# One semaphore per ring slot, and a table stored pair by pair, in a graph network kernel

## The reference

```python
deg = segment_sum(ones, dst) + 1; dinv = rsqrt(deg)
h0 = dinv * (segment_sum(dinv[src] * x[src], dst) + dinv * x) @ W + b + t_emb @ Wt + bt
x = layernorm(x + h0)
mean(v) = segment_sum(v[src], dst) / max(cnt, 1)
h = relu(mean(x) @ Wl1.T + b1 + x @ Wr1.T)
x = layernorm(x + mean(h) @ Wl2.T + b2 + h @ Wr2.T)
```

## Time and profile before

| | |
|---|---|
| median of three runs | 3865.3 us (3864.66 to 3870.44) |
| the profiled execution's own time | 3868.9 us |
| its span, first to last instruction | 3867.1 us |
| first gather issued | 192.15 us |
| PE busy | 3067.6 us (79%) |
| DVE busy | 1094.8 us (28%) |
| ACT busy | 503.1 us (13%) |
| POOL busy | 2257.4 us (58%) |
| moved | 1102.5 MB, 285 GB/s over the span |

### The profile page before, as it was taken

One profiled execution on the slowest core, in us unless ns is written; L12 is line 12 of the kernel. 1 busy time (PEld: TensorE's weight loads), 2 busy tenths in 40 slices (PEclk: granted clock), 3 DMA queues, 4 the chain that ended last, 5 costly groups with the idle time before them and its releaser, 6 DMA issues.

```text
span 3867.1 us, 52767 instructions
## 1 busy us (share of the span) xinstructions
PE 3067.6 (79%) x11711; PEld 1400.9 (36%) x12104; DVE 1094.8 (28%) x1877; ACT 503.1 (13%) x1048; POOL 2257.4 (58%) x2367
## 2 busy tenths in 40 slices
PE   7156667778888878788989978886778889988888
PEld 7012223333333333333444433342334344433333
DVE  8701112222333431112222323332122222222222
ACT  0500000111112220000111111111000111111112
POOL 0066666666666636666666666654666666666663
PEclk9988878888899989899999989998889999999999
DMA  5587788888999968888889999987888888888785
GB/s 170 218 301 273 267 274 289 297 305 308 321 323 324 328 244 286 279 282 277 298 309 309 319 328 321 318 311 262 282 278 284 272 281 278 285 280 280 270 279 192
DMA packets 278572, 1102.52 MB, mean 285 GB/s; under 512 B 53626, under 2 KB 55196, under 8 KB 278514
## 3 DMA queue, kind: packets, MB, share of 16 engines
q0 software_dynamic: 187680, 922.63, 69.3%
q10 hardware_dynamic: 64638, 137.22, 10.0%
q1 hardware_dynamic: 26228, 42.34, 3.1%
HBM read 1003.75 MB, written 99.06 MB: 285 GB/s over the span
## 4 chain that ended last, share of the span: by engine, by line
PE 44%; another core or an unknown queue 20%; issue 19%; ACTq 6%; DVE 3%; ACT 3%; DMA 3%; POOL 2%; DVEq 0%; SPq 0%; POOLq 0%
PE sum_ps L1187 27%; PE root_ps L1195 8%; PE prod_ps L1195 7%; POOL raw L457 2%; DMA raw<-table,idx_ring 1%; ACTq L249 1%; PE selfT_ps L1209 1%; PE aggT_ps L1173 1%; ACT selfT L931 1%; ACTq L969 1%; DMA table<-stage 1%; DVE left_of L643 1%; DVE stage L635 1%; ACTq L272 1%
## 5 line engine op out<-in xcount | busy, mean ns | idle before, releaser
L457 POOL DMA_INDIRECT raw<-table,idx_ring x2346 | 2248.0, 958 | 1483.8 <-issue 834.8
L1187 PE MATMUL sum_ps<-raw,oh 128*128 128x512 bf16 x6682 | 1718.1, 402 | 516.4 <-issue 463.6
L1187 PEld LDWEIGHTS sum_ps<-raw,oh 128*128 128x128 bf16 x7038 | 696.1, 102 | 1434.3 <-issue 778.6
L765 DVE TENSOR_TENSOR oh<-iota_ps,dst_rel 128x1280 bf16<-128x1280 f32 x237 | 352.9, 1489 | 1438.5 <-remote 684.2
L1195 PE MATMUL prod_ps<-W,aggT 128*128 128x512 f32 x1176 | 547.4, 607 | 20.9 <-issue 11.8
L1195 PE MATMUL root_ps<-W,selfT 128*128 128x512 f32 x800 | 400.6, 644 | 72.3 <-issue 69.1
L1195 PEld LDWEIGHTS prod_ps<-W,aggT 128*128 128x128 f32 x1176 | 230.3, 197 | 265.9 <-issue 247.4
L887 ACT ACTIVATE aggT<-aggT_ps 128x512 f32<-128x512 f32 x147 | 87.7, 597 | 1827.0 <-remote 1359.9
L1187 PE MATMUL sum_ps<-raw,oh_next 128*128 128x512 bf16 x847 | 229.8, 401 | 37.7 <-issue 26.8
L1195 PEld LDWEIGHTS root_ps<-W,selfT 128*128 128x128 f32 x800 | 160.6, 206 | 270.2 <-issue 258.9
L924 ACT ACTIVATE selfT<-selfT_ps 128x512 f32<-128x512 f32 x100 | 59.7, 597 | 1004.3 <-remote 644.6
(11 more groups left out here) (149 smaller groups left out, 1156.5 us busy)
## 6 DMA issues: line engine op xcount, KB each, us to landing
raw<-table,idx_ring POOLq DMA_INDIRECT x2346
table<-planes ACTq DMA_DIRECT2D x89, 384.0 KB
selfbuf<-rows ACTq DMA_DIRECT2D x104, 256.0 KB
selfbuf<-table ACTq DMA_DIRECT2D x50, 384.0 KB
table<-stage SPq DMA_DIRECT2D x7, 2688.0 KB, 8.3
rows<-X ACTq DMA_DIRECT2D x49, 256.0 KB
X<-rows ACTq DMA_DIRECT2D x49, 256.0 KB
X<-in_x SPq DMA_DIRECT2D x6, 2048.0 KB
```

The costliest lines, as they stand in the source:

```text
L457: nc.gpsimd.indirect_dma_start(out=raw[:, n, j, :], out_offset=None, in_=tables[L][:, :], in_offset=bass.IndirectOffsetOnAxis(ap=idx_ring[ ...
L765: v.tensor_tensor(oh[:, which * HR:(which + 1) * HR, :, :].rearrange("p n j e -> p (n j) e"), iota_ps[:, 0:P].unsqueeze(1).to_broadcast([P ...
L1187: last = mm(bank, of[:, j, :], raw[:, n, j, p * D:(p + 1) * D], start=fresh, stop=False, skip_group_check=True)
```

## The change

1. `slot_read[n]` takes the place of `pe_done`: PE's last matmul of a group raises the semaphore of its slot, and POOL, DVE and ACT wait for that of the slot that they need.
2. PE waits for `slot_full[n]` itself; SP's loop and `gathered` are gone. `oh_made` is raised by 1 a half block, and PE waits for it at slots 0 and 5 only. ACT's index copy waits until PE has read slot 9 of its block (before: until that slot had landed).
3. The first table is stored in 28 DMAs, one after each of the 28 steps.
4. The edge tables are copied by ACT, after its step 15; the tile ends' counts come after DVE's step 11 and not 8, the column numbers after step 18, and the relative targets after the last step.
5. DVE makes the first one-hots before it waits for the stores. `dst_f` and `ended_f` move in SBUF to where `oh` lies, and `rel_f` is gone.
6. ACT takes a root of one column before it waits for the degrees; DVE's wait for POOL's last constants moves behind the copies that don't need them.

```diff
+            for n, (first, many) in enumerate(TWOS):
+                b, k = first // BT, first % BT
+                sp.wait_ge(S["staged"], n + 1)
+                sp.dma_start(tables[0][first * P:(first + many) * P, :].rearrange("(t p) (a d) -> p t a d", p=P, a=PLANES),
+                             stage[:, b % 2, k:k + many, :, :]).then_inc(stored[b % 2], 16)
...
-                def landed(blk, n):
-
-                    fills = NBLK + 1 if n == 0 else NBLK
-                    sp.wait_ge(slot_full[n], blk * (16 * CH) + 16 * CH * (fills * L + 1))
-                    sp.sem_inc(S["gathered"], 1)
...
-                        pool.wait_ge(S["pe_done"], blk * SLOTS + (REAL * L + n + 1))
+                        pool.wait_ge(slot_read[n], blk + (fills(n, L) + 1))
...
-            dve.wait_ge(S["consts_made"], 3)
             link(v.tensor_copy(cnt[:, :], hist_ps[:, 0:T]))
...
+            dve.wait_ge(S["consts_made"], 3)
...
-                if n == 12:
-                    edge_tables()
-                if n == 16:
-                    relative_targets()
+                if n == 11:
+                    tile_end_counts()
+                if n == 18:
+                    column_numbers()
             low_planes(len(TWOS) - 1)
+            relative_targets()
             dve.wait_ge(S["tabs_made"], 2)
-            dve.wait_ge(S["b0_all_ps"], 1)
-            dve.wait_ge(S["stage_stored0"], 16 * 4)
-            dve.wait_ge(S["stage_stored1"], 16 * 3)
...
-                half_block(0, slice(0, HR * CH), REAL * L + SLOTS)
+                half_block(0, slice(0, HR * CH), slot_read[0], fills(0, L) + 1)
+                if L == 0:
+                    dve.wait_ge(S["b0_all_ps"], 1)
+                    dve.wait_ge(S["stage_stored0"], 16 * 4 * PAIRS)
+                    dve.wait_ge(S["stage_stored1"], 16 * 3 * PAIRS)
...
             act.wait_ge(S["consts_made"], 1)
+            a.activation(sqsum[:, 0:1], eps[:, 0:1], ACT.Sqrt)
...
+            def edge_tables():
+
+                act.wait_ge(S["src_ps"], 1)
+                a.activation(idx_tab[:, 0:4 * CQ], tmp_ps[0][:, 0:4 * CQ], ACT.Copy)
+                a.activation(idx_tab[:, 4 * CQ:NC], tmp_ps[1][:, 0:NC - 4 * CQ], ACT.Copy).then_inc(S["tabs_made"], 1)
+                act.wait_ge(S["dst_ps"], 1)
+                a.activation(dst_f[:, 0:4 * CQ], tmp_ps[2][:, 0:4 * CQ], ACT.Copy)
+                a.activation(dst_f[:, 4 * CQ:NC], tmp_ps[3][:, 0:NC - 4 * CQ], ACT.Copy).then_inc(S["tabs_made"], 1)
...
-                    act.wait_ge(S["gathered"], b * SLOTS + (REAL * L + SLOTS))
+                    act.wait_ge(slot_read[SLOTS - 1], b + (fills(1, L) + 2))
                     next_indices(b % 2, (b + 2) % (NBLK + 1))
...
-                    pe.wait_ge(S["oh_made"], g + (HR * (NW + 1) * L + 1))
-                    pe.wait_ge(S["gathered"], g + (REAL * L + 1))
+                    if n % HR == 0:
+                        pe.wait_ge(S["oh_made"], b * (SLOTS // HR) + ((NW + 1) * L + n // HR + 1))
+                    pe.wait_ge(slot_full[n], b * (16 * CH) + 16 * CH * (fills(n, L) + 1))
```

More of the change, by code:

```diff
@@ L49, in gnn_resnorm @@
     TWOS = [(t, min(2, T // 7 - t % (T // 7))) for t in range(T) if t % (T // 7) % 2 == 0]
+    PAIRS = len(TWOS) // 7
+    assert len(TWOS) == 7 * PAIRS
     HB = 34
@@ L118, in gnn_resnorm @@
         mid = ExitStack()
+        dst_f = sb("dst_f", [P, NC], fp32, mid)
+        ended_f = sb("ended_f", [P, SB * P], fp32, mid)
+        assert 4 * (NC + SB * P) <= 2 * SLOTS * CH * P + 2 * CH * P
         stage = sb("stage", [P, 2, BT, PLANES, D], bf16, mid)
@@ L195, in gnn_resnorm @@
         slot_full = [sem(f"slot_full{n}") for n in range(SLOTS)]
+        slot_read = [sem(f"slot_read{n}") for n in range(SLOTS)]
         block = ctx.enter_context(nc.Block())
@@ L204, in tile_of_x, with fills @@
             return X2[:, bass.ds(t1 * D - D, D)]
+        def fills(n, L):
+            return L * (NBLK + (n == 0))
         def column(per_node, t1):
@@ L349, in _ @@
             stored = (S["stage_stored0"], S["stage_stored1"])
[L350 to L353, removed]
+            for n, (first, many) in enumerate(TWOS):
[3 more added lines that the diff above has]
+                             stage[:, b % 2, k:k + many, :, :]).then_inc(stored[b % 2], 16)
             sp.wait_ge(S["tabs_made"], 2)
             sp.wait_ge(S["b0_made"], 1)
-            sp.wait_ge(S["stage_stored0"], 16 * 4)
-            sp.wait_ge(S["stage_stored1"], 16 * 3)
+            sp.wait_ge(S["stage_stored0"], 16 * 4 * PAIRS)
+            sp.wait_ge(S["stage_stored1"], 16 * 3 * PAIRS)
             for L in range(NL):
@@ L385, in _ @@
                     load_weights(1, wr2t, "wr_loaded")
[L386 to L389, removed]
         @block.gpsimd
@@ L760, in tile_end, with half_block @@
                         dve.nop()
-                def half_block(which, cols, done):
-                    dve.wait_ge(S["pe_done"], done)
+                def half_block(which, cols, read, times):
+                    dve.wait_ge(read, times)
                     v.tensor_tensor(
@@ L867, in _ @@
                     middle_planes(n - 1)
+                if n == 15:
+                    edge_tables()
             middle_planes(len(TWOS) - 1)
@@ L1085, in _ @@
             pe.sem_inc(S["root_ready"], 1)
-            pe.sem_inc(S["pe_done"], SLOTS)
+            for n in range(SLOTS):
+                pe.sem_inc(slot_read[n], 1)
             pe.sem_inc(S["next_used"], 1)
@@ L1229, in groups, with group @@
                             each(pe, rounds[n // HR], rounds[n // HR + 1], lambda r: own_rows(L, r), T + 1)
-                        group(b * SLOTS + n, n, ends[n], ends[n + 1])
-                def group(g, n, first, end):
-                    pe.wait_ge(S["oh_made"], g + (HR * (NW + 1) * L + 1))
-                    pe.wait_ge(S["gathered"], g + (REAL * L + 1))
+                        group(b, n, ends[n], ends[n + 1])
+                def group(b, n, first, end):
+                    if n % HR == 0:
+                        pe.wait_ge(S["oh_made"], b * (SLOTS // HR) + ((NW + 1) * L + n // HR + 1))
+                    pe.wait_ge(slot_full[n], b * (16 * CH) + 16 * CH * (fills(n, L) + 1))
                     with pe.If(end > first):
@@ L1241, in group @@
                         mm(sums_of(L, end + 1, 1), zeros[:, :], zeros[:, 0:1], start=False, stop=False,
-                           skip_group_check=True).then_inc(S["pe_done"], 1)
+                           skip_group_check=True).then_inc(slot_read[n], 1)
                     with pe.Else():
-                        add_rows(sums_of(L, first + 1), oh[:, n, :, :], n, False).then_inc(S["pe_done"], 1)
+                        add_rows(sums_of(L, first + 1), oh[:, n, :, :], n, False).then_inc(slot_read[n], 1)
                     pe.nop()
@@ L1249, in _ @@
                 ends = ended_before(mybir.EngineType.PE, TAIL_GROUP, 1)
-                group(TAIL_GROUP, 0, ends[0], ends[1])
+                group(NBLK, 0, ends[0], ends[1])
                 weigh(L, T - 1)
```

46 lines of the change are left out of this document (16 added, 30 removed).

## The result

The changed kernel takes **3826.8 us** (3825.7 to 3830.7) against 3867.7 us (3864.7 to 3870.4) for the kernel before on the same chip: ratio 0.9891, 95% interval 0.9876 to 0.9906, so 41 us less. I had forecast 3850, 15.6 us less. The sign holds, and the time lies in the stated range of 3812 to 3872, but not in the forecast's own of 3838 to 3857: the gain is over twice the size.

A forecast was written before the change was run, and what follows sets the result against it. No engine was full: DVE bounded the plane loop, and in the layers engines waited for each other through ten slots. 1.6 + 10 + 4.0 = 15.6 us before the gathers and 0 in the layers gave 3850 us, range 3812 to 3872.

The forecast's parts named there:

- Front: Before the plane loop: early dummy Sqrt hides a 1.28 us table load, DVE's moved wait gives 0.35; sum 1.6 us.
- Plane loop: DVE making the first table's planes: stalls 4.2, tile counts 3.5, edge tables 2.0, relative targets 2.15; 11.85, taken as 10 us.
- Last store: Between last subtraction and first gather: only one tile's store follows the last pair, not a batch; gain 4.0 us, bounds 3 and 5.
- Before the gathers: Sum of front 1.6, plane loop 10 and last store 4.0: 15.6 us, between 10 and 18.
- The layers: Three layers of gathers after the first gather: relay, PE's waits, index copy and slot semaphores sum to 0, bounds -27 and +29.
- the ring: Ten gather slots shared by POOL and PE in the layers; their changed waits and semaphores were put at 0 us in sum.
- One wait less for PE: In eight of ten groups of the layers PE drops one event instruction, median 51 ns; taken as nothing.
- SP's relay: SP waited for each of 1173 groups and passed it on to PE; removing it was taken as 0 to 1 us.
- Rival 1: Layers: PE's shorter control path saves 27 us, giving 3823; sign: PE's unnamed waits below 465 us; chance 0.22.
- Rival 2: Block starts in the layers: POOL waits for ACT's index copy, 39 exposed starts cost 29 us, giving 3879; chance 0.12.
- Rival 3: Plane loop: stores per pair don't overlap, the last ends about 14 us later, giving 3880; chance 0.05.
- Rival 4: Layers: a different phase gives back as much as the early start gains, 3865, within 0.2%; chance 0.11.

The follow-up runs named there:

- kind A: Chips on which the kernel before takes 3833 to 3880 us, as on the one of the forecast.
- a store per batch: Changed kernel with the first table stored in seven batches of seven tiles, as before: 0.9927 of the kernel before, on a slow chip (3880.1 us before).
- the four waits: Changed kernel plus four waits on PE before every group, on semaphores reached long ago: 0.9932 of the kernel before, on a slow chip.
- kind B: Chips on which the kernel before takes 3323 to 3327 us.
- run 5: Not a run: in "seven batches that each run 5 to 6 us over 9.1", "run" is a verb and 5 to 6 us a time.
- the ring alone: Kernel before with only SP's relay, PE's waits, slot semaphores and index copy changed: 0.9995, 0.9998 and 1.0004 of the kernel before, on fast chips.
- the start alone: Kernel before with every edit ahead of the gathers and the old slot signalling: 0.9945, 0.9943 and 0.9947 of the kernel before, on fast chips.

## Why the prediction was right in sign and wrong in size

*Front, 1.6 us:* 1.8. The table load is gone from behind the histogram, and DVE's copy stands at 95.70, released by PE: 0.50 us earlier, where 0.35 was forecast. The other 1.3 are the load.

*Plane loop, 10 us:* 11.7. The three waits and the moved work are gone as named. What was mis-sized is the 1.6 us that I let come back as a stall on ScalarE's edge tables: the row at 140.93 has 0.29. 11.85 - 0.29 = 11.6. ScalarE itself waited 13.8 us for VectorE in the loop, so it had room for four copies, as its 53.26 busy us of 77.82 had said; I let the stall come back in spite of them. I also summed terms that hang together (stores and order), which was right only because both were changed.

*Last store, 4.0 us:* 4.5. The last landing released ACT at 173.17, 4.0 us after the last subtraction's end at 169.13; 4.3 was expected. The Trainium skill's *DMA: Bandwidth & Descriptors*, in the section on where the ~2 µs goes, gives a DMA a fixed cost of about 2 us, fitted there to DMAs that GpSimd issues, where these stores are SP's. By that rule with nothing overlapped 21 more stores would lose. The runs bear out the overlap: with 28 stores the first gather comes 13.1 us earlier than with seven, and a landing takes 2.4 to 3.4 us.

*Before the gathers, 15.6 (10 to 18):* 17.9, as the first gather shows, and all of it arrives at the end.

*The layers, 0:* 23 to 24 us on chips of kind A, in three comparisons (23.0 and 23.8 for the changed kernel, 24.0 with a store per batch). That these belong to the ring is inferred, from kernels that all have both parts: the start's part of each is the time of its first gather, and it arrives in full. A gain that needs ring and start together isn't excluded. **The step that failed is the zero for the layers**, and in it first this term: "*One wait less for PE* in eight of ten groups: its event instruction has a median of 51 ns, in a sequencer that runs ahead of the matmuls: I take nothing", together with the 0 to 1 us for SP's relay. I took a median from a line whose longest was 713 ns, and showed no row for the sequencer that runs ahead. The trace of the kernel before does bear it out, but only narrowly: the instructions of that line end 0.23 us (median) before the matmul then in flight, by the profile's modelled ends. A standstill of 0.7 us, as that line has, is longer than this lead.

What the runs show in its place: on chips of kind A about 13 of the 24 us hang on PE's way into a group. Whether it is the relay's later signal or PE's own instructions isn't settled: instructions alone can cost as much, as the four waits show, and SP's relaying instructions, too, last up to 713 ns in the kernel before. On kind B the same edits measure nothing. The other 10 us remained in both kernels, whose slots are still given back by a semaphore each and whose index copy is ordered as in the change. That the giving back or the copy, both also put at nothing, is their cause was not tried on such a chip; where these 10 us come from stays open.

*Rival 1* (PE's control path, 27 us, 3823) had the right place and nearly the time, but not by its own arithmetic: one sixteenth of PE's unnamed waits, which fell by 4 us (425.7 to 421.4) and, with the waits for landings, not at all. Its sign in the profile, those waits below 465, came true (421.4) for a reason of naming. *Rival 2* (POOL behind the index copy): 3.7 us in 7 waits, against 4.5 in 6; refuted. *Rival 3* (stores don't overlap): refuted. Its own sum was loose as well: four times 3.8 us are 15, not 14, and seven batches that each run 5 to 6 us over 9.1 would add more than the 14 us it names. *Rival 4* (the early start isn't kept): refuted by the 13.1 and 12.9 us.

## What to carry to other kernels

Find out whether the kernel runs alike on every chip before a difference is explained: the same edits were worth 23 to 24 us in the layers on one kind and nothing on the other. A control instruction ahead of an engine's work is not to be put at nothing by its median alone; read the longest duration of its line too. Where that line had 51/51/51 ns the whole ring edit gave nothing, where it had 2/51/713 up to 24 us. A store in pieces and less work for the engine that feeds it are worth more together (16 us) than alone (8.5 for the pieces, 3.0 for the order), so decide on them together. If a sign is to tell two theories apart, take one that doesn't change its name when semaphores are renamed, such as an engine's whole idle time.

## What the chips showed that I had not expected

The kernel before takes 3868 us on the chip of the forecast, whose number isn't known, 3833, 3871 and 3880 on three numbered ones, and 3323 to 3327 on seven others. All of the difference lies in the layers: the first gather of the ring alone is at 191.94 us on kind B, that of the kernel before at 192.15 on kind A. The mean granted clock of PE is 0.909 to 0.917 in the profiles of kind A and 0.968 to 0.983 in those of kind B. The lower clock may be a cause or a consequence of PE's standing still; no run tells. It isn't what the change gained, for it is 0.916 in the profile before and 0.917 in that after. The window from 200 to 600 us in the start alone and in the kernel with a store per batch has

```profile
200.00:600.00 400.00, 279.13 (x1116) 106.53 (x1116) 71.93 (x103) 18.28 (x46) 302.55 (x321) 0.97 0.93 327
```

```profile
200.00:600.00 400.00, 250.78 (x873) 94.23 (x914) 49.14 (x61) 9.22 (x25) 261.21 (x276) 0.82 0.82 279
```

first the one on kind B, then the one on kind A: 1116 weight loads against 914. On kind A the weight loads of the gathered groups (`raw`), where one directly follows another, come over 0.55 us apart 176 to 244 times a run, most often by 0.7, 1.4, 2.1 or 2.8 us; in the traces of kind B not once. What stops PE's queue, and ScalarE's, in such steps on some chips is open; no run here reaches it.
